# Output projection that waits by sequence and opens with its bias row, and attention products ahead of the transposes of the widened sums, in a float32 kernel of four attention layers

## What is computed

```python
def attention(q, k, v, src_mask, dam, zero_pad, gammas):
    ...                                            # softmax, cumulated sums, distance effect
    scores = jax.nn.softmax(scores, axis=-1)       # the second softmax
    if zero_pad:
        scores = scores.at[:, :, 0, :].set(0.0)
    return jnp.einsum('bhqk,bhkd->bhqd', scores, v)

def transformer_layer(bmask, query, key, values, apply_pos, p):
    ...
    concat = att.transpose(0, 2, 1, 3).reshape(Bb, Ss, Dd)
    q2 = concat @ p['oW'].T + p['ob']              # the output projection
    x = layernorm(query + q2, p['ln1_g'], p['ln1_b'])
    if apply_pos:
        ff = jax.nn.relu(x @ p['w1'].T + p['b1']) @ p['w2'].T + p['b2']
        x = layernorm(x + ff, p['ln2_g'], p['ln2_b'])
    return x

y = transformer_layer(1, qa, qa, qa, True, P(0))   # layer 0, with feed-forward
x = transformer_layer(1, q, q, q, False, P(1))     # layer 1, without
x = transformer_layer(0, x, x, y, True, P(2))      # layer 2, with feed-forward
# then cross-attention of x over the context: softmax(q k / 4) v, @ wo + bo, layernorm
```

## Time and profile before

| What | Value |
|---|---|
| median of three runs | 3154.62 us (3153.51 to 3154.82) |
| the profiled execution | 3153.52 us, its span 3151.7 us |
| TensorE (PE) busy | 2861.6 us, 91% of the span |
| VectorE (DVE) busy | 2761.0 us, 88% |
| ScalarE (ACT) busy | 2677.6 us, 85% |
| GpSimd (POOL) busy | 717.0 us, 23% |
| chain that ended last | DVE 42%, PE 39%, issue 13%, ACT 2% |

### The profile page before, as it was taken

One profiled execution on the slowest core, in us unless ns is written; L12 is line 12 of the kernel. 1 busy time (PEld: TensorE's weight loads), 2 busy tenths in 40 slices (PEclk: granted clock), 3 DMA queues, 4 the chain that ended last, 5 costly groups with the idle time before them and its releaser, 6 DMA issues.

```text
span 3151.7 us, 77324 instructions
## 1 busy us (share of the span) xinstructions
PE 2861.6 (91%) x21912; PEld 2123.1 (67%) x21912; DVE 2761.0 (88%) x5898; ACT 2677.6 (85%) x10212; POOL 717.0 (23%) x1116
## 2 busy tenths in 40 slices
PE   5799999999999999999999999999999999999996
PEld 3566676676676676676676676676677676667664
DVE  4689998889998889998889998889998889998883
ACT  2688998888998888988888988888988888988882
POOL 1112212222222222222222222222221222221220
PEclk8799999999999999999999999999999999999997
DMA  5000111100111100111101011111011110011100
GB/s 176 26 21 25 33 32 34 31 24 24 31 31 34 31 25 23 31 31 34 31 26 29 24 31 35 30 28 30 21 30 35 30 34 24 22 30 35 32 18 11
DMA packets 167469, 101.13 MB, mean 32 GB/s; under 512 B 37312, under 2 KB 166908, under 8 KB 167420
## 3 DMA queue, kind: packets, MB, share of 16 engines
q1 hardware_dynamic: 158668, 90.83, 10.3%
q10 hardware_dynamic: 8752, 9.71, 0.9%
HBM read 56.84 MB, written 10.01 MB: 21 GB/s over the span
## 4 chain that ended last, share of the span: by engine, by line
DVE 42%; PE 39%; issue 13%; ACT 2%; SPq 2%; DMA 1%; POOL 1%; DVEq 1%; POOLq 0%
PE gen_ps L644 13%; PE gen_ps L793 7%; DVE X L998 6%; DVE E L989 5%; PE scores_ps L690 5%; DVE nm L1014 4%; DVE nm L981 4%; DVE X L1008 4%; DVE res L1039 3%; DVE res L1052 3%; PE gen_ps L700 3%; PE gen_ps L741 2%; PE gen_ps L717 2%; PE gen_ps L652 2%; DVE moments L1049 2%
## 5 line engine op out<-in xcount | busy, mean ns | idle before, releaser
L857 ACT ACTIVATE X<-X,nm 128x128 f32<-128x128 f32 x1536 | 594.5, 395 | 47.3 <-DVE nm L1014 47.3
L857 ACT ACTIVATE E<-scores_ps,nm 128x128 f32<-128x128 f32 x1536 | 537.5, 381 | 92.0 <-DVE nm L981 92.0
L981 DVE TENSOR_REDUCE nm<-scores_ps 128x8 f32<-128x1024 f32 x320 | 389.6, 1218 | 115.1 <-PE scores_ps L690 115.0
L644 PE MATMUL gen_ps<-f_buf,up_w 128*128 128x256 f32 x2048 | 475.9, 386 | 0.9 <-DVE f_buf L470 0.9
L793 PE MATMUL gen_ps<-down_w,hidden 128*128 128x256 f32 x2048 | 452.7, 379 | 1.0 <-DVE hidden L497 1.0
L644 PEld LDWEIGHTS gen_ps<-f_buf,up_w 128*128 128x128 f32 x2048 | 380.8, 191 | 98.4 <-issue 50.9
L1135 POOL TENSOR_SCALAR_AFFINE_SELECT X<-X 128x1024 f32<-128x1024 f32 x192 | 210.3, 1095 | 1037.6 <-DVE X L1008 1037.6
L989 DVE TENSOR_TENSOR_SCAN E<-chain,E 128x1024 f32<-128x1024 bf16 x192 | 429.6, 2237 | 0.0
L998 DVE SCALAR_TENSOR_TENSOR X<-E,rz,decay 128x128 f32<-128x128 f32 x1536 | 424.0, 346 | 2.1 <-DVE E L989 0.5
L793 PEld LDWEIGHTS gen_ps<-down_w,hidden 128*128 128x128 f32 x2048 | 384.2, 190 | 51.0 <-DVE hidden L497 1.4
L857 ACT ACTIVATE X<-scores_ps,nm 128x128 f32<-128x128 f32 x1024 | 359.4, 397 | 53.1 <-DVE nm L981 50.6
(11 more groups left out here) (142 smaller groups left out, 5248.2 us busy)
## 6 DMA issues: line engine op xcount, KB each, us to landing
k_diag<-k_f SPq DMA_DIRECT2D x768, 32.0 KB, 1.9
xk_diag<-xk_f SPq DMA_DIRECT2D x1024, 8.0 KB, 1.7
ctx_f<-in_ctxT SPq DMA_DIRECT2D x32, 256.0 KB, 2.7
x_f<-in_xT SPq DMA_DIRECT2D x32, 256.0 KB, 2.7
ctx_t<-in_ctx SPq DMA_DIRECT2D x32, 256.0 KB, 3.6
x_t<-in_x SPq DMA_DIRECT2D x32, 256.0 KB, 3.7
cx_f<-in_ctxT SPq DMA_DIRECT2D x32, 256.0 KB, 2.9
out<-out_t SPq DMA_DIRECT2D x32, 256.0 KB, 2.2
```

Source lines behind the costliest of these rows:

```text
L644: mm = nc.tensor.matmul(ps[:, i * T:(i + 1) * T], w[:, k, c * P:(c + 1) * P], src[:, k, :], start=(k == 0), stop=(k == C - 1))
L857: a = nc.scalar.activation(dst[:, cols], src[:, cols], ACT.Exp, bias=minus_max[:, h:h + 1], accum_out=sums[:, h:h + 1])
L981: nc.vector.tensor_reduce(nm1[:, UNIT[u], :], unit_heads(scores_ps[SLOT[u]][:, :]), AX_X, ALU.max, negate=True).then_inc(max1_done, 1)
```

## The change

In `attend` the wait for `wide_done` and the transposes of the widened sums move behind the products; the last transpose now says `gen_full`. In `out_proj` the two bias rows of layers 0 and 1 become one bfloat16 matmul of 512 columns over both sequences, and it opens the step. The sequences are then taken in the order in which their units stand in TensorE's list (`att_order`), and each sequence waits for its own units alone. The lists, banks and all other steps stay.

```diff
+att_order = kind_order(TENSOR, "att")
...
                 in_sbuf(now, d, ("att", u), value_step, ("pt", u, 0), ("pt", u, 1))
-                pe.wait_ge(wide_done, wide_order.upto(now, d, ("widen", u)))
-                for c in range(C if is_layer(u) else 1):
-                    first = (C if is_layer(u) else 1) + c
-                    nc.tensor.transpose(ps[:, first * S:(first + 1) * S], rz_wide[:, W_SLOT[u], c * P:(c + 1) * P], ident[:, :])
                 if is_layer(u):
...
+                pe.wait_ge(wide_done, wide_order.upto(now, d, ("widen", u)))
+                for c in range(C if is_layer(u) else 1):
+                    first = (C if is_layer(u) else 1) + c
+                    mm = nc.tensor.transpose(ps[:, first * S:(first + 1) * S], rz_wide[:, W_SLOT[u], c * P:(c + 1) * P], ident[:, :])
                 return mm
...
-                in_sbuf(now, d, ("o", l), *[("att", u) for u in SLOT if u[0] == l])
                 w, att = (o_w[l], att_f[l % 2]) if l < L else (xo_w, xatt_f)
-                for b in range(G):
+                if l < 2:
+                    nc.tensor.matmul(ps[:, :], ones3[:, :],
+                                     row_bias[:, O_ROWS[l], :].unsqueeze(1).to_broadcast([P, G, D]), start=True, stop=False)
+                units = [step[1] for step in sorted((step for _, step in att_order.events if step[1][0] == l),
+                                                    key=lambda step: (att_order.late[step], att_order.index[step]))]
+                batches = [units[0][1]] + [b for b in range(G) if b != units[0][1]]
+                assert units[-1][1] == batches[-1]
+                for b in batches:
                     out = ps[:, b * D:(b + 1) * D]
+                    in_sbuf(now, d, ("o", l), *[("att", u) for u in units if u[1] == b])
                     for c in range(C):
-                        mm = nc.tensor.matmul(out, att[:, b, c, :], w[:, c, :], start=(c == 0), stop=(c == C - 1 and l > 1))
-                    if l < 2:
-                        mm = add_row(out, O_ROWS[l])
+                        mm = nc.tensor.matmul(out, att[:, b, c, :], w[:, c, :], start=(c == 0 and l > 1),
+                                              stop=(c == C - 1 and (l > 1 or units[-1][1] == b)))
                 return mm
```

More of the change, by code:

```diff
@@ L716, in attend @@
                             i = next(i for i in range(UH) if head_at(i) == h)
-                            mm = nc.tensor.matmul(ps[j * DK:(j + 1) * DK, c * S:(c + 1) * S],
+                            nc.tensor.matmul(ps[j * DK:(j + 1) * DK, c * S:(c + 1) * S],
                                                   v_t[u[0]][:, b, h * DK:(h + 1) * DK],
@@ L724, in attend @@
                             v = xv_t[:, b, u[2] * 4 + pair, e, :, :].rearrange("p e d -> p (e d)")
-                            mm = nc.tensor.matmul(ps[pair * 32:(pair + 1) * 32, 0:S], v,
+                            nc.tensor.matmul(ps[pair * 32:(pair + 1) * 32, 0:S], v,
                                                   probs_f[:, P_SLOT[u], h * S:(h + 1) * S], start=(e == 0), stop=(e == 1))
+                pe.wait_ge(wide_done, wide_order.upto(now, d, ("widen", u)))
+                for c in range(C if is_layer(u) else 1):
+                    first = (C if is_layer(u) else 1) + c
+                    mm = nc.tensor.transpose(ps[:, first * S:(first + 1) * S], rz_wide[:, W_SLOT[u], c * P:(c + 1) * P], ident[:, :])
                 return mm
```

## The result

| | before | after |
|---|---|---|
| median | 3154.82 us (3148.75 to 3157.27, 20 runs) | 3166.07 us (3155.29 to 3170.91, 20 runs) |
| ratio | | 1.003 (95%: 1.0023 to 1.0037) |
| profiled execution | 3153.52 us, span 3151.7 | 3168.99 us, span 3167.3 |
| mean granted clock | 0.977 | 0.969 |

The change costs 0.3%, about 11 us of the median and 15.6 us of the profiled span. The forecast was 3168, by falls of TensorE's clock (stretches in which the granted clock is 0.50), and the trace shows such falls. The profiled execution of the kernel after is one of its slower ones: it lies 2.9 us above the median, with the lowest mean clock of the twenty (the others read 0.970 to 0.981).

A forecast was written before the change was run, and what follows sets the result against it. No engine bounds everywhere: VectorE covers TensorE until 1515.69, then TensorE sets the turn. 20 x 1.1 - 10 x 0.32 - 3.5 = +15.3 us, so 3168 us; range 3139 to 3184, the forecast's own 3161 to 3186.

The forecast's parts named there:

- The mechanism: Ahead of `turn(2,2)`: `o(0)` ends 0.35 us sooner, idle grows from 1.66 to about 2.0 us, TensorE's clock falls there.
- The signs listed for "right": Expected in the profile: `att(1,1)` without POOL's wait, 512-column bias row, 2.0 us pause, `q` over 2.5 us, turns 95.3 or 93.9.
- The count: Number of loop turns with a clock fall at `turn(2,2)`: 20 of 30 taken; 14 or more given 0.55.
- the old pair of pauses: Before's waits of 0.69 and 1.14 us around `att(0,0)`, ahead of `o(0)`; the clock fell in 10 of 30 turns.
- The first rival: The clock stays up behind the 2.0 us pause: -13 us, 3141 us; chance of being faster by over 0.2%: 0.27.
- Few falls: Falls as often as before but now on the path: +1 us, 3155 us; chance 0.18, shared with a lost lead.
- falls in most turns: Falls in all 30 turns: +30 us, 3184 us, the forecast's upper end; 14 or more falls have chance 0.55.
- The edit is not what it says: The projection still waits for the whole pair of multiplications through its bank; lead below 0.1 us; no chance of its own.
- Price of a fall: 3.3 us at half clock behind the pause at `turn(2,2)`: +1.1 us a turn against before (0.8 to 1.3).
- Turns without a fall: Loop turns at full clock save 0.22 us in `att(1,1)` plus 0.10 us in `o(1)`, 0.32 us together.
- Ends of the run: Ramp (`att` waits for POOL) about -2 us, drain (`o(2)`, `o(3)`) -1.8 us; taken as -3.5 us (0 to -4).
- half of which can run in the wait: In the drain, half of the eight matmuls of `o(2)` and `o(3)` (1.97 and 1.99 us) run during the wait: -1.8 us.

The follow-up runs named there:

- undo_o0: Kernel after, but layer 0's projection waits for both sequences first and ends with its two bias rows, as before; 3146.01 us, ratio 0.997.
- fill4: Kernel after plus four unread matmuls of 512 columns ahead of the wait for x_tok in `turn(2,2)`; 3143.46 us, ratio 0.9958.
- b_nobias0: Kernel before without the two bias rows of layer 0's projection; 3168.02 us, ratio 1.0044.
- p2_projection: Kernel after with the old order in `attend` (transposes ahead of products), so the projection change alone; 3165.95 us, ratio 1.0039.
- p1_products: Kernel before with only the new order in `attend` (products ahead of the wait and transposes); 3149.18 us, ratio 0.9979.
- fill1: Kernel after plus one unread matmul of 512 columns ahead of the wait in `turn(2,2)`; 3152.62 us in one execution.
- b_fill4: Kernel before plus four unread matmuls of 512 columns ahead of the wait for x_tok in `turn(2,2)`; 3159.65 us, ratio 1.002.

## Why the prediction was right, and where its terms were off

**The mechanism held.** The projection that ends sooner made the pause longer, the clock fell behind the longer pause, and the falls cost time because TensorE carries the stretch behind it; undo_o0, fill4 and b_nobias0 each show one side of this. A turn with a fall was put at 95.3 us and measured 95.12; one without at 93.9, and measured 93.90. The pause was put at 2.0 us and became 2.09: `o(0)` starts 0.33 us sooner relative to `turn(2,2)` (4.21 us ahead of it instead of 3.88 in the earlier trace rows) and, opened by the bias row, takes 0.10 us less. The signs listed for "right" are there: `att(1,1)` without POOL's wait, one row of 512 columns ahead of `o(1)`, the longer pause, the stretches at 0.50, and the two lengths of a turn. One holds in part: `q` takes over 2.5 us in 16 of the 21 slow turns. In the other five, where the stretch opens within 0.1 us of the start of `turn(2,2)`, it takes 2.26 to 2.35.

**The count was luck in part.** Forecast were 20 falls in 30 turns, a choice between the 10 of the old pair of pauses and all 30; 21 came in the profiled execution. p2_projection, with the same pause, had 13 in its 28 whole turns. What sets the number isn't shown, and the falls of the other nineteen executions of after are not on record; all of them read a higher mean clock, so the median probably stands for fewer.

**The first rival** (the clock stays up, 3141 us) fell with the stretches at 0.50, but its size was about right: fill4, in which the clock does stay up in all whole turns, took 3143.46. **Few falls** is ruled out by the count, **falls in most turns** too, though 20 of 28 is not far from it. **The edit is not what it says** fell with the pause, which grew by 0.43 us.

**The Trainium skill** ("TensorE: Matmul & The Clock Gate", section "HAM oscillation — how this bites in real kernels") has waits between bursts of matmuls bring the half-rate clock back; the 21 stretches at 0.50 behind a wait of 2.09 us agree. The waits in that section's own case are longer than this one, so it bears out the direction and does not by itself give the forecast's sum, as the prediction has it.

**The pause and the falls.** By the whole turns of the nine profiled executions there is no fall at `turn(2,2)` behind a pause of 1.66 us or less; behind 1.87 us there is one in 28 turns, behind 1.88 eleven, behind 2.09 thirteen and twenty.

**Terms that were off:**
- *Price of a fall.* Forecast were 1.1 us above before's turn and 1.1 + 0.32 = 1.42 above a turn without a fall; after shows 0.98 and 1.22, so the term was some 0.1 to 0.2 us too high.
- *Turns without a fall.* The two terms were nearly right one by one: p1_products measured 0.27 us for `att(1,1)` (forecast 0.22), p2_projection 0.07 for `o(1)` (0.10). Together they should give 0.34, and after shows 0.24. What is missing goes with a stall in the dense stretch, between `scores(2,1)` and the `up` step behind it. The first two lines are of before, the last two of after:

```profile
1543.02 1.09 PE L690 MATMUL scores_ps<-k_diag,k_f 64*64 64x256 f32 x16
1544.04 1.99 PE L644 MATMUL gen_ps<-f_buf,up_w 128*128 128x256 f32 x8
...
1547.50 1.27 PE L691 MATMUL scores_ps<-k_diag,k_f 64*64 64x256 f32 x16
1548.70 1.99 PE L645 MATMUL gen_ps<-f_buf,up_w 128*128 128x256 f32 x8
```

  From start to start that is 1.16 to 1.24 us in 25 of after's turns, 1.18 in the mean (and 1.17 to 1.23 in 27 each of undo_o0 and fill1), against 1.02 in all turns of before, p1_products, p2_projection, fill4 and the other two. The turn of fill4, 93.73 us, is 0.41 below before's and so has the whole gain. fill4 differs from after by four matmuls at another place. That the stall hangs on the position of the code would fit this, but no run tests it, and what it waits for isn't shown. It costs after at most 25 x 0.16 = 4.0 us.
- *Ends of the run.* Forecast -3.5, measured -3.16 + 1.24 = -1.9. In the drain `o(2)` starts with 0.14 us of idle instead of 1.07, as expected, but the cross projection still waits 0.75 us against 0.79 before, and one long stall is new:

```profile
3068.50 1.13 PE L645 MATMUL gen_ps<-f_buf,up_w 128*128 128x256 f32 x4 [1.77 <-issue]
...
3094.12 1.98 PE L749 MATMUL gen_ps<-o_w,att_f 128*128 128x256 f32 x8
...
3158.38 1.99 PE L749 MATMUL gen_ps<-xo_w,xatt_f 128*128 128x256 f32 x8 [0.75 <-DVE xatt_f L467]
```

  One term failed: "half of which can run in the wait", for the cross projection. The step's bank is also that of `att(3,1,0)`, a step of the second sequence, so the first sequence can't open it sooner. The question was asked of `o(0)`'s bank, and not of this one. And "issue" means that TensorE waited for nothing that the profile shows. By and large the nine drains are longer where such a stall is longer:

| | p2_projection | b_nobias0 | before | after | b_fill4 | fill1 | p1_products | undo_o0 | fill4 |
|---|---|---|---|---|---|---|---|---|---|
| drain, us | 144.0 | 142.5 | 144.2 | 145.4 | 147.0 | 147.9 | 146.6 | 147.3 | 149.1 |
| longest such stall, us | none | none | 0.49 | 1.77 | 2.08 | 2.43 | 3.15 | 3.12 | 3.06 |

  In fill4 the clock fell behind it, and the eight matmuls of an `up` step, 1.99 us elsewhere, took 3.53:

```profile
3038.01 0.66 PE L691 MATMUL scores_ps<-k_diag,k_f 64*64 64x256 f32 x7 [3.06 <-issue]
3038.60 3.53 PE L645 MATMUL gen_ps<-f_buf,up_w 128*128 128x256 f32 x8
```

  The drain's code runs once. The stall stands 43 to 47 us into the drain, in three kernels ahead of an `up` step and in three ahead of the products of a `scores` step. Without its 1.77 us and the fall at `turn(2,2)` that lies in after's drain (about 1 us) the drain would be 142.7 us, 1.5 below before's, which has 0.49 us of such a stall itself; the forecast was -1.8. That sum is argued, not measured.
- *The ramp's -3.2* is not shown to be the work of `att`: p1_products has the same `att` and its whole turns begin at 371.67 us (before: 371.44), and fill1, which has after's ramp but for one matmul a turn, begins at 373.64. Two of fill1's ramp turns have a fall, one of after's and none at that place in p1_products, so the ramps differ in more than `att`. The forecast of -2 looks right here by chance.

The errors nearly cancelled. For the profiled execution the falls were put 22 - 19.6 = 2.4 us too high, and the gains too high as well: 3.2 us instead of 1.9 in the turns without a fall, 3.5 instead of 1.9 at the ends. So the +15.3 us of the forecast against +15.6 of the two spans is closer than its terms; the medians differ by 11. The sign rested on two things. That the longer pause stands ahead of the stretch that TensorE carries was read from the rows; that more than nine falls would come of it was a guess, and it came true.

## What to carry to other kernels

A step that ends sooner is no gain when the next one waits for another engine: it makes one longer pause, and on TensorE a pause right ahead of the stretch that TensorE carries can cost more than the step saved. Before an edit shortens TensorE's work next to a wait, add up the pause that results and look in the trace for the longest pause behind which the granted clock stayed at 1.00 in every turn. If the new one is longer, the clock may fall, though here it did so in only one turn of 28 at 1.87 us. Then leave the step late, or put matmuls into the pause, and check that the stretch ahead can't be slowed so that they run past the wait.

## What was not expected of the hardware

- From 1.66 to 1.88 us of pause, 0.22 us more, the falls at `turn(2,2)` go from none to eleven in 28 turns. But 1.87 us in fill1 had one. Besides 0.01 us of pause the two kernels differ in what runs ahead of it (the wait ahead of `o(0)` is 1.14 us in b_nobias0 and 0.89 in fill1, and fill1 has the filler), and in the length of a turn without a fall (94.11 and 93.87 us). Which of these counts isn't shown.
- The falls come in a regular order, with the same pauses in turns with and without one. At `o(0)` they come in every second turn of p1_products and in every fifth of b_fill4; undo_o0 has none in its first thirteen whole turns and then one in every second. fill1's fall is in its first whole turn, and the 27 behind it have none. So what the pause leaves open is not chance from turn to turn. What sets the order isn't shown.
- Taking matmuls out made the kernel before slower by 0.44% (b_nobias0), and adding matmuls whose result nobody reads made the changed kernel the fastest of the nine, 0.42% below before (fill4).
- The same fall costs 0.00 us in `o(0)` (8 turns of before, 14 of p1_products, 8 of undo_o0), 0.38 us when fillers stand behind it (b_fill4) and 1.0 to 1.2 us at `turn(2,2)`. The mean granted clock of a run (0.973 in p1_products, 0.977 in before) doesn't tell which: p1_products has the lower clock and the shorter time.
- TensorE stalls of about 0.16 us a turn in the loop and up to 3.15 us in the drain appeared and went with edits far from them, with no engine and no DMA named as what ended them. The gain that was to be judged is 0.34 us a turn, so two kernels that differ by a single step can differ by half of that for this reason alone.
